# Moving batch 1's first projections ahead of the maxima, and the normalisations from ScalarE to GpSimd, in a decoder layer

## The chip, the core and the metric
The kernel runs on one NeuronCore of a Trainium2 chip. Its engines are TensorE (matmuls and transposes; PE in the profile, its weight loads PEld), VectorE (DVE), ScalarE (ACT), GpSimd (POOL) and SyncE (SP), which only issues copies here. Each runs its own list of instructions in order, and they meet at semaphores. "ACTq" and "SPq" are an engine's queue: what it issues or handles beside its arithmetic. The metric is the device time of one execution in microseconds; lower is better.

## What is computed
One decoder layer on x (4 batches, 256 rows, 256 channels) and a context of the same shape, all float32:

```
x = layernorm(x + attention(x))        # 32 heads of 8 channels, 8 key/value heads, biases
x = layernorm(x + wkv(w, u, k=x, v=ctx))
x = layernorm(x + ffn(x))              # ffn has a layernorm of its own, gamma and beta
attention: softmax(Q K^T / sqrt(8)) V, then Wo and bo
wkv:  a scan over the rows, per channel, with running maximum o:
      y = (exp(o-no) p + exp(u+k-no) v) / (exp(o-no) q + exp(u+k-no))
ffn:  layernorm(relu(x up_w)^2 down_w + (x expert_weight) * sum(top 2 of x gate_w)) * gamma + beta
```

## The kernel before
**Units.** The attention of a batch is cut into two groups of 128 query rows, so there are 8 groups, and a group into 16 units of two matmuls for maxima and one for exponentials. `maxima_unit` (L589) multiplies q by k for the query rows and VectorE takes the row maxima (L1180), negated. `exp_unit` (L605) multiplies k by q again, transposed, and ScalarE exponentiates into one of 8 `probs` buffers (L812). `pv_group` (L617) multiplies four of them by v. The exponential of a unit comes LAG = 15 units behind its maxima. While there are no exponentials yet, an idle matmul (L635) stands behind each maxima unit.

**Precision and rows.** q and k are split into three bfloat16 parts, and the six products that matter lie in rows 0 to 5 of every 8 partitions of `q_rows` and `k_rows` (BLOCKS, written by `q_row_copies` and `k_row_copies`, L486 and L492, as copies from `q_parts` and `k_parts`). Row 6 of `q_rows` takes the negated maxima of the group: VectorE's or GpSimd's `parts` (L1218, L1037) cut them in parts, TensorE transposes them (`m`, L692), VectorE or ScalarE takes them out (`mt`, L1228, L861), SyncE copies them into the row (`mc`, L550). There are two such parcels for each group. Every batch has its own `q_rows` and `k_rows`, set to zero and one by memsets, most of them on GpSimd. The row copies of a batch are issued by SyncE; for batch 0 some of them by ScalarE (L819, L824).

**Chunks.** Behind the attention each group of 128 rows is a chunk that goes through out projection, layernorm 0, the scan, layernorm 1, the feed-forward part and layernorms 2 and 3. WIDE is 6: chunks 0 to 5 are the early ones. For a layernorm k, VectorE takes statistics (`st`, L1145) and the variance (`var`, L1152, L1154), GpSimd raises it to the power -1/2 (`pow`, L1061); for an early chunk it also makes the negative mean (L1059) and the offset (L1066), and ScalarE normalises (`nor`, L794). The last two chunks are normalised by VectorE (L1160).

**Order.** All engines walk through the same ticks. The table `AT` gives each step of each batch, group or chunk a tick, and an engine's instructions are in the order of the ticks; units have theirs every R = 32 ticks from START = 1920, the exponentials 480 later. So the order of work on each engine, the SyncE queue with its loads (`load`) among it, is written out by hand or by a planner. `LOAD_AFTER` makes some loads wait for a count of maxima. The single PSUM bank `ps_a` is handed from use to use in the order of the ticks (A_BY). Before the first maxima unit TensorE waits for the parts and rows of batch 0 with 2, 12 and 2 idle matmuls between the waits.

Of the kernel before, what the change touches and what calls it, by code (L numbers as in the profile page):

```python
# [6 lines left out]
def decoder_layer(nc, x, x_cols, ctx_cols, w_qk, w_post, up_w, down_w, out):  # L7
    fp32, bf16 = mybir.dt.float32, mybir.dt.bfloat16
# [42 lines left out]
        "k": (1456, 2315, 2440, 3400),  # L51
        "kv": (-1, 2342, 2463, 3423),
        "k1": (1514, 2367, 2505, 3466),
        "kr": (1542, 2381, 2625, 3501),
        "vc": (1610, -1, -1, -1),
        "k2": (1580, 2527, 3002, 3551),
        "k3": (1661, 2784, 3522, 3773),
        "q0": (1503, 2379, 2792, 3624),
        "qs0": (-1, 2399, 2875, 3647),
        "qh0": (1561, 2540, 2904, 3685),  # L60
        "qr0": (1589, 2556, 3075, 3742),
        "qm0": (1618, 2603, 3177, 4479),
        "ql0": (1643, 2641, 3398, 4558),
        "q1": (1561, 2536, 2920, 3560),
        "qs1": (-1, 2559, 2975, 3583),
        "qh1": (1803, 2716, 3023, 4019),
        "qr1": (1831, 2748, 3052, 4075),
        "qm1": (1860, 2801, 3092, 4264),
        "ql1": (1885, 2922, 3110, 4538),
        "kc0": (1542, 2381, 3240, 4435),  # L70
        "kc1": (1634, 2637, 3618, 4606),
        "kc2": (1703, 2805, 3852, 4658),
        "qc00": (1644, 2556, 3102, 4698),
# [4 lines left out]
        "qc12": (1989, 3087, 3963, 4919),  # L78
        "load": (2110, 2145, 2179, 2324, 2683, 2857, 3075, 3295, 3839, 3867, 3910, 3941, 3993, 4675),
# [17 lines left out]
        "att": (3119, 3916, 4333, 4751, 5167, 5656, 6186, 6734),  # L97
        "att_e": (3135, 4030, 4319, 4735, 5182, 5662, 6175, 6760),
        "xbo": (2985, 3148, 3697, 4454, 5032, 5129, 5552, 6707),
# [1354 lines left out]
```

## Time and profile before

| what | value |
|---|---|
| median of 3 runs | 216.61 us (215.62 to 217.32) |
| the profiled execution | 216.79 us |
| its span, first to last instruction | 215.0 us |
| TensorE busy | 199.7 us (93%) |
| VectorE busy | 163.1 us (76%) |
| ScalarE busy | 150.9 us (70%) |
| GpSimd busy | 129.6 us (60%) |

Busy is time in which an instruction of the engine was running, by the profile; the ends of matmuls are modelled. The profiled execution is one run; what lies between its span and its time is start and end around the instructions.

### The profile page before, as it was taken

Reading aid. Unit: us, or ns where it says so; the run is one execution under the profiler, and the core shown is the slowest. Engines: PE = TensorE matmul, PEld = TensorE weight load, DVE = VectorE, ACT = ScalarE, POOL = GpSimd, SP = SyncE. Lnnn points to the kernel's source line nnn. Section 1 sums busy time; section 2 is a strip of 40 time slices with the busy share of each in tenths; the row PEclk is TensorE's granted clock in tenths of the full one; section 3 lists DMA queues with packets and bytes.
Section 4 is the critical chain, followed back from the end, with each engine's and each line's share of the span. In section 5 each row is a group of like instructions: output and inputs, shape, how many; then the busy total and the mean of one; then the engine's idle time right before and its main releaser. Section 6 shows DMA issues by size and latency. Waiting matters only on the chain.

```text
span 215.0 us, 4364 instructions
## 1 busy us (share of the span) xinstructions
PE 199.7 (93%) x1295; PEld 111.7 (52%) x1295; DVE 163.1 (76%) x392; ACT 150.9 (70%) x334; POOL 129.6 (60%) x256
## 2 busy tenths in 40 slices
PE   8889999979999899999999999999999998799970
PEld 3533543433433334575465445664655487698950
DVE  3469778778999899998979899976754837956274
ACT  2310477867899789989799879998967984763520
POOL 8995164753465724567476786867495493177622
PEclk9999999999999999999999999999999999999996
DMA  3145227943116602131000000010000000000001
GB/s 122 43 117 170 70 56 226 255 127 108 27 44 203 218 2 64 49 90 36 19 9 7 2 0 9 2 33 25 2 6 0 3 24 26 2 5 0 24 24 49
DMA packets 14759, 12.35 MB, mean 57 GB/s; under 512 B 3856, under 2 KB 12688, under 8 KB 14480
## 3 DMA queue, kind: packets, MB, share of 16 engines
q1 hardware_dynamic: 14064, 11.72, 19.0%
q10 hardware_dynamic: 672, 0.36, 0.6%
q8 instruction: 10, 0.16, 0.3%
q14 instruction: 13, 0.11, 0.2%
HBM read 6.57 MB, written 1.05 MB: 35 GB/s over the span
## 4 chain that ended last, share of the span: by engine, by line
PE 71%; DMA 8%; DVE 7%; ACT 6%; issue 5%; ACTq 1%; POOL 1%; POOLq 0%; DVEq 0%
PE ps_b L781 10%; PE ps_heads L629 10%; PE ps_exp L613 10%; PE ps_b L764 9%; DMA q_rows<-max_t 7%; PE ps_max L600 6%; PE ps_exp L635 4%; PE ps_exp L764 3%; PE ps_b L747 3%; PE ps_a L722 3%; PE ps_a L676 2%; ACT probs L812 2%; PE ps_a L665 2%; DVE maxima L1180 2%; PE ps_a L585 2%
## 5 line engine op out<-in xcount | busy, mean ns | idle before, releaser
L1180 DVE TENSOR_REDUCE maxima<-ps_max 128x2 f32<-128x512 f32 x128 | 85.0, 684 | 10.6 <-PE ps_max L600 9.7
L812 ACT ACTIVATE probs<-ps_exp 128x512 f32<-128x512 f32 x128 | 73.6, 599 | 14.6 <-PE ps_exp L613 14.1
L613 PE MATMUL ps_exp<-q_rows,k_rows 64*128 64x512 bf16 x128 | 46.2, 385 | 3.8 <-ACT probs L812 1.7
L600 PE MATMUL ps_max<-k_rows,q_rows 64*128 64x256 bf16 x256 | 47.4, 274 | 0.7 <-DMA q_rows<-q_parts 0.6
L613 PEld LDWEIGHTS ps_exp<-q_rows,k_rows 64*128 64x128 bf16 x128 | 11.4, 93 | 45.0 <-ACT probs L812 25.9
L629 PE MATMUL ps_heads<-probs,v_cols 128*32 128x512 f32 x256 | 33.9, 604 | 0.0
L781 PE MATMUL ps_b<-down_sb,inner_t 128*128 128x256 f32 x112 | 29.4, 388 | 0.7 <-ACT relu_t L943 0.7
L764 PE MATMUL ps_b<-x_t,up_sb 128*128 128x128 f32 x192 | 27.1, 285 | 1.1 <-DVE h L1367 1.1
L1061 POOL TENSOR_TENSOR rstd<-var_eps,minus_half 128x1 f32<-128x1 f32 x32 | 19.6, 611 | 11.7 <-DVE var_eps L1154 11.7
L764 PEld LDWEIGHTS ps_b<-x_t,up_sb 128*128 128x128 f32 x192 | 23.2, 191 | 6.0 <-issue 4.0
L781 PEld LDWEIGHTS ps_b<-down_sb,inner_t 128*128 128x128 f32 x112 | 19.4, 190 | 4.3 <-issue 1.5
L1145 DVE BATCH_NORM_STATS2 stats<-h 128x6 f32<-128x256 f32 x32 | 13.4, 422 | 8.1 <-POOL h L1129 7.7
L600 PEld LDWEIGHTS ps_max<-k_rows,q_rows 64*128 64x128 bf16 x256 | 14.6, 94 | 6.4 <-DVE maxima L1180 3.9
L1059 POOL TENSOR_SCALAR neg_mean<-mean_var 128x1 f32<-128x1 f32 x24 | 6.3, 262 | 17.9 <-DVE var_eps L1154 17.8
L1074 POOL TENSOR_TENSOR new_v<-wgt,ctx_t 128x256 f32<-128x256 f32 x14 | 10.4, 741 | 4.9 <-issue 3.9
L1037 POOL TENSOR_TENSOR maxima<-maxima 128x16 f32<-128x16 f32 x28 | 6.3, 225 | 9.6 <-DVE maxima L1180 8.4
L898 ACT ACTIVATE wgt<-delta,bonus_decay 128x128 f32<-128x128 f32 x32 | 10.9, 400 | 0.7 <-DVE delta L1276 0.5
L980 POOL MEMSET q_rows<- 128x4096 bf16 x3 | 10.5, 3511 | 0.0
L905 ACT ACTIVATE wgt<-wgt 128x512 f32<-128x512 f32 x16 | 10.2, 636 | 0.1
L1090 POOL TENSOR_TENSOR y_num<-wgt,num 128x256 f32<-128x256 f32 x8 | 5.6, 699 | 7.3 <-DVE num L1305 7.3
L949 ACT ACTIVATE inner_t<-relu_t 128x512 f32<-128x512 f32 x16 | 9.9, 627 | 0.1
L635 PE MATMUL ps_exp<-ident_bf 128*128 128x512 bf16 x31 | 9.5, 384 | 0.0
(129 smaller groups left out, 345.2 us busy)
## 6 DMA issues: line engine op xcount, KB each, us to landing
q_rows<-q_parts SPq DMA_DIRECT2D x46, 64.0 KB, 2.1
x_t<-in_x_cols SPq DMA_DIRECT2D x4, 256.0 KB, 3.3
x_in<-in_x SPq DMA_DIRECT2D x4, 256.0 KB, 4.5
ctx_t<-in_ctx_cols SPq DMA_DIRECT2D x4, 256.0 KB, 3.0
up_sb<-in_up_w SPq DMA_DIRECT2D x1, 1024.0 KB, 6.1
down_sb<-in_down_w SPq DMA_DIRECT2D x1, 1024.0 KB, 6.1
out_y<-y_out SPq DMA_DIRECT2D x8, 128.0 KB, 1.7
post_sb<-in_w_post SPq DMA_DIRECT2D x1, 906.0 KB, 5.5
```

The lines of the kernel that those rows point to most:

```text
L600: last = nc.tensor.matmul(ps_max[n % 2][:, r, :], q_rows[b][at:at + HALF, g, REP * jj + 2 * half + r, h * P:h * P + P], k_rows[b][at:at + ...
L613: nc.tensor.matmul(ps_exp[n % 2][:, :], k_rows[b][at:at + HALF, JH * g + jj, kt * P:kt * P + P], q_rows[b][at:at + HALF, g, REP * jj:REP * ...
L629: last = nc.tensor.matmul(ps_heads[s % 2][32 * j:32 * j + 32, :], flat(v_cols[b][:, :, :])[:, at:at + 32], probs[(4 * n + j) % 8][:, :], s ...
L635: nc.tensor.matmul(ps_exp[1][:, :], src[:, 0:P], src[:, 0:P].rearrange("p (a t) -> p a t", a=1) .broadcast_to([P, REP, P]), start=True, st ...
L764: last = nc.tensor.matmul(ffn_banks[k][:, v * n:v * n + n], up_sb[:, c, m * P:m * P + P], x2_t[:, c, columns_of(p)], start=(c == 0), stop= ...
L781: last = nc.tensor.matmul(down_part(p, i), inner_t[:, m, i * P:i * P + P], down_sb[:, m, :], start=(m == 0), stop=(m == NI - 1))
L812: nc.scalar.activation(probs[n % 8][:, :], ps_exp[n % 2][:, :], ACT.Exp, scale=SCALE).then_inc(s_exp, 1)
L898: last = nc.scalar.activation(wgt[:, 2 + i, c, cols], delta[:, c, cols], ACT.Relu, scale=sign, bias=bonus_decay[:, i, c:c + 1])
L980: gp.memset(q_rows[b][:], 0.0).then_inc(s_ones, 1)
L1061: gp.tensor_tensor(rstd[k][:, ti], var_eps[k][:, ti], minus_half[:, ti], ALU.pow).then_inc(s_rstd[k], 1)
L1145: own(nc.vector.bn_stats(stats[k][:, i, :], src[:, i, :]))
L1180: nc.vector.tensor_reduce(maxima[s % 2][:, g, j // JH, 0, at:at + 2], ps_max[n % 2][:, :, :], AX, ALU.max, negate=True).then_inc(s_max, 1)
```

## The change
- The k projection of batch 1 and its first q projection stand before the first maxima unit; x of batch 1 is loaded third, at once. Three idle matmuls each stand behind batch 1's k, batch 0's second q and batch 0's v; the 16 idle matmuls between the waits go.
- GpSimd normalises the six early chunks, four times each. VectorE no longer adds the epsilon for them, GpSimd does; negative mean and offset go.
- GpSimd issues the row copies of the second and third part of batch 0's k (three copies). ScalarE issues three q copies of set 0, SyncE the rest.
- There are three `q_rows` and `k_rows` instead of four. Batch 3 takes batch 0's place, after its exponentials, and a copy for each set clears row 6 first. `q_rows` 1 is cleared by VectorE.
- There are 12 `probs` buffers instead of 8.
- For group 0, GpSimd makes the parts of the maxima and ScalarE takes the transposed ones out (VectorE before); ScalarE takes out batch 0's v.
- All ticks are new. x of batch 1 leaves the list of loads; the steps named in the prediction are shown.

```diff
 AT
-        "k": (1456, 2315, 2440, 3400),
+        "k": (1474, 1618, 2440, 3304),
-        "kv": (-1, 2342, 2463, 3423),
+        "kv": (-1, 1678, 2463, 3327),
-        "k2": (1580, 2527, 3002, 3551),
+        "k2": (1588, 2286, 3037, 3707),
-        "q0": (1503, 2379, 2792, 3624),
+        "q0": (1520, 1820, 2792, 3624),
-        "qh0": (1561, 2540, 2904, 3685),
+        "qh0": (1605, 1913, 2872, 3687),
-        "qc01": (1771, 2697, 3344, 4508),
+        "qc01": (1698, 2314, 3617, 4825),
-        "qc02": (1737, 2830, 3655, 4911),
+        "qc02": (1762, 2779, 3568, 4878),
-        "qc10": (1831, 2869, 3550, 4417),
+        "qc10": (1989, 2849, 3684, 5037),
-        "qc11": (1931, 2937, 3184, 4896),
+        "qc11": (1894, 2680, 3312, 5017),
-        "load": (2110, 2145, 2179, 2324, 2683, 2857, 3075, 3295, 3839, 3867, 3910, 3941, 3993, 4675),
+        "load": (2165, 2199, 2234, 2617, 2917, 2945, 3124, 3380, 3584, 3652, 3839, 5410, 5430),
-        "vb": (1903, 2623, 2687, 4223),
+        "vb": (1795, 2687, 3007, 4095),
-        "mc0": (2311, 2785, 3329, 3804, 4393, 4880, 5290, 5906),
+        "mc0": (2287, 2797, 3297, 3824, 4367, 4810, 5374, 5850),
-        "mc1": (2534, 3055, 3532, 4102, 4591, 5104, 5640, 6183),
+        "mc1": (2534, 3050, 3553, 4079, 4640, 5120, 5671, 6080),
...
+    ROT = 3
+    NPROBS = 12
...
 SyncE
+            def rows_free(b):
+                sp.wait_ge(s_ones, ROT + (b >= 2))
+                if b == 1:
+                    sp.wait_ge(s_q1_zero, 1)
+                if b >= ROT:
+                    sp.wait_ge(s_exp, UNITS * TT * (b - ROT + 1))
...
+                                if b >= ROT and qp == 0:
+                                    sp.dma_start(row_block(q_rows[b % ROT][:, g], len(BLOCKS)),
+                                                 row_block(q_rows[1][:, g], len(BLOCKS) + 1)).then_inc(s_rows[b][g], 16)
...
 ScalarE
-                    if n >= 8:
-                        act.wait_ge(s_pv, (n - 8) // 4 + 1)
+                    if n >= NPROBS:
+                        act.wait_ge(s_pv, (n - NPROBS) // 4 + 1)
...
 GpSimd
+            for kp, done in ((1, s_k2), (2, s_k3)):
+                gp.wait_ge(done, 1)
+                k_row_copies(gp, 0, kp, s_krows_pool)
+            gp.memset(q_rows[2][:], 0.0).then_inc(s_ones, 1)
...
+            def normalise(k, p, src, dst, done):
+                gp.wait_ge(s_rstd[k], p + 1)
+                for i in CHUNKS[p][1]:
+                    last = gp.tensor_scalar(dst[:, i, :], src[:, i, :], mean_var[k][:, i, 0:1], rstd[k][:, i:i + 1],
+                                            ALU.subtract, ALU.mult)
+                last.then_inc(done, 1)
...
                             if p < WIDE:
-                                gp.tensor_scalar(neg_mean[k][:, ti], mean_var[k][:, ti, 0], -1.0, None,
-                                                 ALU.mult).then_inc(s_negmean[k], 1)
+                                gp.tensor_scalar(var_eps[k][:, ti], mean_var[k][:, ti, 1], EPS, None,
+                                                 ALU.add).then_inc(s_pool, 1)
+                                npool[0] += 1
+                                gp.wait_ge(s_pool, npool[0])
                             gp.tensor_tensor(rstd[k][:, ti], var_eps[k][:, ti], minus_half[:, ti],
                                              ALU.pow).then_inc(s_rstd[k], 1)
-                            if p < WIDE:
-                                gp.wait_ge(s_negmean[k], p + 1)
-                                gp.wait_ge(s_rstd[k], p + 1)
-                                gp.tensor_tensor(offset[k][:, ti], neg_mean[k][:, ti], rstd[k][:, ti],
-                                                 ALU.mult).then_inc(s_offset[k], 1)
...
 TensorE
-                    if n == 0:
-
-                        for done, value, n_idle in ((s_q2[0], 1, ROW_FILL), (s_q3[0], 1, 6 * ROW_FILL),
-                                                    (s_krows[0], 16 * len(BLOCKS), ROW_FILL)):
-                            pe.wait_ge(done, value)
-                            for k in range(n_idle):
-                                idle_matmul(ident_bf)
```

## Rows read from the trace of the kernel before

**Rows 1.** four stretches: busy us (count) by engine, granted TensorE clock, DMA share, GB/s
```profile
0.00:24.80 24.80, 22.36 (x94) 10.04 (x94) 15.25 (x29) 4.31 (x8) 18.93 (x30) 1.00 0.38 110
24.80:80.00 55.20, 51.28 (x374) 20.98 (x373) 47.46 (x92) 44.41 (x97) 28.61 (x64) 1.00 0.43 125
80.00:180.00 100.00, 99.10 (x668) 57.01 (x667) 80.21 (x208) 86.50 (x198) 66.83 (x133) 1.00 0.08 20
180.00:215.00 35.00, 26.90 (x166) 23.73 (x164) 20.17 (x65) 15.66 (x32) 15.23 (x29) 0.94 0.06 20
```

**Rows 2.** TensorE's waits, 24 to 80 us: in total, times, longest
```profile
PE ps_exp L613 <- ACT probs L812: 1.7, 7, 0.3
PE ps_exp L613 <- DMA q_rows<-max_t: 1.6, 2, 0.9
```

**Rows 3.** TensorE's waits, 80 to 215 us
```profile
PE ps_b L764 <- DVE h L1367: 1.1, 1, 1.1
PE ps_b L781 <- ACT relu_t L943: 0.7, 1, 0.7
```

**Rows 4.** timeline of the start: start us, us, engine, line, operation, count
```profile
9.12 3.63 PE L635 MATMUL ps_exp<-ident_bf 128*128 128x512 bf16 x16
...
13.29 0.38 PE L600 MATMUL ps_max<-k_rows,q_rows 64*128 64x256 bf16 x2 [0.55 <-DMA q_rows<-q_parts]
...
13.77 6.42 DVE L1180 TENSOR_REDUCE maxima<-ps_max 128x2 f32<-128x512 f32 x10
...
22.64 0.39 PE L600 MATMUL ps_max<-k_rows,q_rows 64*128 64x256 bf16 x2
...
23.29 0.39 PE L600 MATMUL ps_max<-k_rows,q_rows 64*128 64x256 bf16 x2
...
24.80 0.39 PE L600 MATMUL ps_max<-k_rows,q_rows 64*128 64x256 bf16 x2
```

**Rows 5.** timeline before the first unit, ScalarE and the queues
```profile
7.59 0.40 ACT L840 ACTIVATE k_parts<-kv_rest 64x256 bf16<-64x256 f32 x1
...
8.24 0.42 ACT L853 ACTIVATE q_parts<-q_rest 128x256 bf16<-128x256 f32 x1 [0.25 <-DVE q_rest L1194]
8.30 2.09 ACTq L495 DMA_DIRECT2D k_rows<-k_parts  x3
...
8.91 7.12 SPq L489 DMA_DIRECT2D q_rows<-q_parts  x10
...
10.49 1.22 ACTq L489 DMA_DIRECT2D q_rows<-q_parts  x2
11.75 0.47 ACT L849 ACTIVATE q_parts<-ps_heads,qk_sb 128x256 bf16<-128x256 f32 x1 [3.09 <-issue]
```

**Rows 6.** timeline of SyncE's queue, 15 to 26 us
```profile
17.88 0.43 SPq L518 DMA_DIRECT2D ctx_t<-in_ctx_cols  x1
21.41 0.54 SPq L550 DMA_DIRECT2D q_rows<-max_t  x1
```

**Rows 7.** the copies of line 550, issue to landing
```profile
DMA to landing us min/median/max: 1.8/1.9/3.8
```

**Rows 8.** groups of instructions: xcount, then busy us, mean ns, idle before
```profile
L794 ACT ACTIVATE x<-h,offset,rstd 128x256 f32<-128x256 f32 x12 | 7.2, 601 | 0.9 <-POOL offset L1066 0.7
...
L1059 POOL TENSOR_SCALAR neg_mean<-mean_var 128x1 f32<-128x1 f32 x24 | 6.3, 262 | 17.9 <-DVE var_eps L1154 17.8
...
L1066 POOL TENSOR_TENSOR offset<-neg_mean,rstd 128x1 f32<-128x1 f32 x24 | 4.6, 193 | 3.7 <-POOL rstd L1061 0.4
L1125 POOL TENSOR_TENSOR h<-h,post_sb 128x256 f32<-128x256 f32 x6 | 4.4, 730 | 2.1 <-ACT h L794 2.0
...
L1022 POOL CAST q_parts<-q_rest 128x256 bf16<-128x256 f32 x6 | 2.4, 394 | 0.1
```

**Rows 9.** chain that ended last, 24 to 80 us: start us, us, what
```profile
70.87 3.68 DMA q_rows<-max_t
```

**Rows 10.** GpSimd's waits, 24 to 200 us
```profile
POOL maxima L1037 <- DVE maxima L1180: 8.4, 7, 2.6
```

More of the change, by code:

```diff
@@ L263, in decoder_layer @@
         k_rest, v_t = [kv[0:KVD] for kv in kv_rest], [kv[KVD:2 * KVD] for kv in kv_rest]
-        q_rows = [sb(f"q_rows{b}", [P, NSET, HH, T], bf16) for b in range(B)]
-        k_rows = [sb(f"k_rows{b}", [P, NSET * JH, T], bf16) for b in range(B)]
+        q_rows = [sb(f"q_rows{i}", [P, NSET, HH, T], bf16) for i in range(ROT)]
+        k_rows = [sb(f"k_rows{i}", [P, NSET * JH, T], bf16) for i in range(ROT)]
         v_cols = [sb(f"v_cols{b}", [P, TT * NSET, GS * 32 + HS]) for b in range(B)]
@@ L275, in decoder_layer @@
         max_t = sb("max_t", [P, NSET, P], bf16)
-        probs = [sb(f"probs{i}", [P, REP * P]) for i in range(8)]
+        probs = [sb(f"probs{i}", [P, REP * P]) for i in range(NPROBS)]
         heads_t = [sb(f"heads_t{i}", [P, REP * P]) for i in range(2)]
@@ L310, in decoder_layer @@
         rstd = [sb(f"rstd{i}", [P, TT]) for i in range(4)]
-        neg_mean = [sb(f"neg_mean{i}", [P, TT]) for i in range(4)]
-        offset = [sb(f"offset{i}", [P, TT]) for i in range(4)]
         ps_max = [ps(f"ps_max{i}", [P, 2, T]) for i in range(2)]
@@ L357, in decoder_layer @@
         s_var = [sem(f"s_var{k}") for k in range(4)]
-        s_negmean = [sem(f"s_negmean{k}") for k in range(4)]
         s_rstd = [sem(f"s_rstd{k}") for k in range(4)]
-        s_offset = [sem(f"s_offset{k}") for k in range(4)]
         s_x1 = by_class("s_x1")
@@ L600, in maxima_unit @@
                     last = nc.tensor.matmul(ps_max[n % 2][:, r, :],
[L601 to L602 removed]
+                                            q_rows[b % ROT][at:at + HALF, g, REP * jj + 2 * half + r, h * P:h * P + P],
+                                            k_rows[b % ROT][at:at + HALF, JH * g + jj, :], start=True, stop=True)
                 last.then_inc(s_max_mm, 1)
@@ L667, in _ @@
                         last.then_inc(s_a, 1)
+                        if b == 1:
+                            for k in range(FILL):
+                                idle_matmul(ident_bf)
                     for g in range(NSET):
@@ L678, in _ @@
                             last.then_inc(s_q0 if b == 0 else s_a, 1)
+                            if b == 0 and g == 1:
+                                for k in range(FILL):
+                                    idle_matmul(ident_bf)
                     if AT["v"][b] == tick:
@@ L685, in _ @@
                         last.then_inc(s_a, 1)
+                        if b == 0:
+                            for k in range(FILL):
+                                idle_matmul(ident_bf)
                 for s in range(GROUPS):
@@ L837, in _ @@
                                              bias=bkv_sb[0:KVD, 0:1]).then_inc(s_k1, 1)
+                    if b == 0 and AT["vb"][0] == tick:
+                        act.wait_ge(s_const, 1)
+                        a_filled(act, ("v", 0))
+                        nc.scalar.activation(
+                            heads_of(v_cols[0])[:, :, :, 0:HD],
+                            ps_a[:, 0:TT * KVD].rearrange("p (x j d) -> p x j d", j=GS, d=HD), ACT.Copy).then_inc(s_a_read, 1)
                     if b == 0 and AT["k2"][0] == tick:
@@ L968, in _ @@
             gp.memset(k_rows[0][:], 1.0).then_inc(s_ones, 1)
-            for i in range(2):
-                gp.memset(maxima[i][:, :, :, PARTS:HD], 0.0).then_inc(s_zeros, 1)
             own(gp.memset(ident[:], 0.0))
@@ L975, in _ @@
             gp.tensor_copy(ident_bf[:], ident[:]).then_inc(s_ident, 1)
+            for i in range(2):
+                gp.memset(maxima[i][:, :, :, PARTS:HD], 0.0).then_inc(s_zeros, 1)
+            for b in range(1, ROT):
+                gp.memset(k_rows[b][:], 1.0).then_inc(s_ones, 1)
             own(gp.memset(v_cols[0][:], 0.0))
             gp.memset(heads_of(v_cols[0])[:, :, :, HD:HD + 1], 1.0).then_inc(s_const, 1)
+            gp.wait_ge(s_ones, 1)
+            for kp, done in ((1, s_k2), (2, s_k3)):
+                gp.wait_ge(done, 1)
+                k_row_copies(gp, 0, kp, s_krows_pool)
+            gp.memset(q_rows[2][:], 0.0).then_inc(s_ones, 1)
             for b in range(1, B):
-                gp.memset(k_rows[b][:], 1.0).then_inc(s_ones, 1)
-                gp.memset(q_rows[b][:], 0.0).then_inc(s_ones, 1)
                 own(gp.memset(v_cols[b][:], 0.0))
```

181 lines of the change are left out of this document (81 added, 100 removed), and 172 rows, old and new, of the table AT.

## The prediction

> **What bounds the kernel now.** I read the table of stretches first, then TensorE's waits, then the timeline of the first 25 us, and last the groups of instructions and the copies. The table [rows 1] shows TensorE busy 99.1 of the 100 us between 80 and 180, with VectorE at 80.2, ScalarE at 86.5 and GpSimd at 66.8: there the order and amount of TensorE's work is the time, and a faster ScalarE buys nothing by itself. The granted clock is 1.00 up to 180 (the 2.4 GHz level). Room is in three places. Before 24.8 TensorE is busy too, but partly with idle matmuls. From 24.8 to 80 it is idle 55.20 - 51.28 = 3.9 us. After 180 it is idle 8.1 us, nearly all in the last chunk's chain, whose code and order the change leaves as they are.
>
> Of the 3.9 us, TensorE's own waits name 1.7 us for ScalarE's exponentials and 1.6 us for the copy of the maxima into row 6 of `q_rows` [rows 2]; 0.6 us has small causes. Later only two waits stand out, 1.1 us for a VectorE sum and 0.7 us for ScalarE's ReLU [rows 3].
>
> **The first projections of batch 1.** Before, they stand among the first 15 maxima units. Two neighbouring units without a projection start 22.64 and 23.29, 0.65 apart; with one between them 23.29 and 24.80, 1.51 apart [rows 4]. One projection costs 0.86 us there, the two 1.7 us. The change puts k and q0 of batch 1 before the first unit, where TensorE now runs 16 idle matmuls for 3.63 us [rows 4] and then waits: the cover is long enough for both, with 9 idle matmuls left.
>
> **Does the first unit come earlier?** Now it starts at 13.29, 2.19 us after the last of five copies issued by ScalarE's queue: three k copies from 8.30, two q copies from 10.49, 0.61 each, so the last at 11.10 [rows 4, 5]. After, ScalarE issues three q copies alone, but k's second part is written before q's first (0.4 us more), which makes q's second part some 0.7 us later than the 8.24 of now [rows 5]. It ends at 8.24 + 0.7 + 0.42 = 9.36; a dispatch for batch 1 lies between, so the last of three issues starts at about 9.46 + 1.22 = 10.7, and the unit could start at 12.9. Set 0's copies are one half. The projection q0 of batch 1 must wait for ScalarE's new copy of v, behind those issues (until 11.3), 0.45 us, and takes 0.86 to 1.0: it ends at 12.7, just hidden. GpSimd now issues three k copies. No row shows one issued there; at ScalarE's 0.61 the third starts near 9.3, at double that near 10.5, and both land before 12.9: nothing.
>
> The other half is set 1, needed by the ninth unit. ScalarE starts its q at 11.75 now, and SyncE's ten q copies end at 8.91 + 7.12 = 16.03, so the last starts at 15.4 and is usable at 17.6, before the ninth unit at 13.29 + 8 x 0.643 = 18.4 [rows 4, 5]. After, q of set 1 stands behind the same three issues and the copy of v (11.75 again), but SyncE takes its second part first: q, rest and second part end at about 13.2, six issues of 0.61 start the last at 16.3, usable at 18.5. The ninth unit was due at 12.9 + 5.1 = 18.0. So the 0.4 us won at the first unit is lost at the ninth, which starts at 18.5, as now.
>
> **The first exponential.** From the ninth unit to it is 24.80 - 18.4 = 6.4 us now, and 4.7 without the two projections: 23.2. It also needs the first row copy of the maxima. Now that is issued at 21.41, the loads before it at 17.88 and earlier [rows 6]. After, SyncE meets three loads (x_in of batch 0, ctx of batch 0, x of batch 2) ahead of this copy, the first of which waits for the last q copy at 18.5. The row copy goes out near 21.0 behind 768 KB. A row copy lands in 1.8, 1.9 or 3.8 us (least, median, most) [rows 7]: 22.9 to 24.8. I take 23.6, between median and most: a gain of 24.8 - 23.6 = 1.2 us. Its ends are 1.65 (the copy is hidden) and 0 (it lands last at 24.8).
>
> **GpSimd normalises six chunks.** Four normalisations for each of six chunks, 24 activations in three groups of 12, 6 and 6 at 0.60 [rows 8], leave ScalarE: 14.3 us of its 150.9. The same operation on GpSimd has no row. Its nearest ones are the cast of one input, 0.39, and the sum of two, 0.73 [rows 8]; it has one tensor input and two scalars, so I take 0.47, the cast with the 0.07 by which a 128x1 TENSOR_SCALAR (0.262) stands over a 128x1 TENSOR_TENSOR (0.193) there. GpSimd gives up 24 products of 0.193 and exchanges one 0.262 for another: per normalisation +0.28 (bounds +0.20 and +0.54), together +6.7 us over some 190 us. It also drops three memsets at the start. It stays under TensorE's load [rows 1]. Per normalisation the path from variance to result loses a hop and 0.15 of VectorE's. All that is off TensorE's path in the 80 to 180 stretch: 0 there.
>
> **Twelve exp buffers, three places for rows, the new order.** With ScalarE shorter and exponentials allowed four more ahead of the products, some of the 1.7 us goes; with the weight loads moved against the row copies (the third chunk of the order puts `up_w` and x of batch 3 between two copies, `down_w` right behind one) some of the 1.6 us. The chain of waits has a row copy of 3.68 us at 70.87 that TensorE waits for [rows 9]. I take half of 3.3, 1.6 us; ends 0.5 and 2.6. After 80, 0.3 of the 0.7 for ReLU (0 and 0.7).
> Three places cost a new wait in SyncE: batch 3's rows wait for exponential 32 of 128. By the ticks it is due two units after that one, so what is queued behind it (the later row copies) is held for at most a unit: 0, and if it slips, up to 0.7 for TensorE. The copies that clear row 6 are two more on that queue, 0.6 each, hidden by slack of several units.
>
> **The sum.** 215.0 - 1.2 - 1.6 - 0.3 = 211.9 us of span. The profiled execution took 216.79 with a span of 215.0, so 1.79 lies around it: 213.7. The median of the three runs is 216.61, 0.18 below that execution: 213.5 us.
>
> **Rivals.** (A) All the room is taken: 1.65 + 3.9 + 0.7 = 6.25, so 210.4. For it: TensorE's other stretches show that it can run without gaps. Against: the waits of [rows 2] have several causes.
> (B) The moved work is given back to row copies: the first lands at 24.8 and the later ones stay as late; only 0.3 remains, 216.3. For it: SyncE has three loads in front of the first copy, and the longest landing is 3.8 [rows 7].
> (C) GpSimd's queue becomes the wait, the case on the other side. The parts of the maxima stand in it with the normalisations, and transpose, copy and exponentials hang on them. It is idle before these parts 7 times, 8.4 us [rows 10], for 14 parcels: seven come without a margin. If each of the seven stands behind one normalisation and its scalar step, 0.47 + 0.26 = 0.73, TensorE loses 5.1, against the 3.1 gained: 218.6. It decides once more than four of the seven are not covered. Against it: GpSimd waits 8.4 us in the others, and the parcels have slack of about four units.
> (D) The k copies issued by GpSimd land late. If an issue takes 1.8, three times ScalarE's, the third starts at 11.6, the first unit is at 13.8 and the ninth at 18.95: +0.45, so 214.0. The Trainium skill, SBUF — State Buffer, "SBUF: two separate sides", says of copies issued by GpSimd that their descriptors are made by that engine and are held up while VectorE runs in a two-port mode; no row of before has such a copy, so nothing here bears it out yet.
>
> **Chances.** The forecast 0.48, with its own range 211.8 (1.65 + 2.6 + 0.7) to 215.3 (0.8 + 0.5); A 0.09; B 0.20; C 0.15; D 0.08. For the range, from A's 210.4 to 217.5, part of the way to C, about 0.15 is left out. Faster by over 1% (which is about what a measurement can tell from no change) is under 214.4: most of the forecast (0.42), A and half of D: 0.55. Slower is over 218.8: the worse half of C and mishaps of B, 0.12. Within 1%: 0.33.
>
> **What would show it.** The first unit at about 12.9, the ninth at 18.5, the first exponential at 23.6 with a wait for the maxima's row copy ahead of it. TensorE's idle time from there to 80 near 2.3 us. ScalarE at about 137 us of busy time, GpSimd's normalisation at 0.47. TensorE's waits on the parts of the maxima (transposes, L692) would mean C; a first unit at 13.8 with the wait on the k rows, D. If the whole gain is there at 25 us and gone at 80, B. I am wrong altogether if TensorE's busy time in the later stretches grows by more small changes between its kinds of work, which no wait would show.

## The result and the profile after

The kernel after takes 222.11 us (221.18 to 222.24), the one before 216.29 in the same job: the ratio is 1.025 [1.019, 1.032], slower by 1.9 to 3.2%. Forecast were 213.5 us and a range of 210.4 to 217.5. The profiled execution took 221.18 us, with a span of 219.3 against 215.0. Times here are medians of undisturbed executions; one execution each of the kernel after, of e3 and of e14 was disturbed and is left out, and the profile of e3 is of that one.

The table below is read from the timelines, one profiled execution for each kernel: the start in us of the first, 65th, 97th, 113th and last of the 128 exponentials on ScalarE, and the span. The labelled kernels come in the next section.

| kernel | 1st | 65th | 97th | 113th | last | span |
|---|---|---|---|---|---|---|
| before | 25.3 | 84.8 | 124.6 | 147.5 | 170.1 | 215.0 |
| after | 22.8 | 80.5 | 120.7 | 148.3 | 171.2 | 219.3 |
| e9_copy_for_norm | 23.1 | 80.5 | 119.4 | 143.7 | 166.6 | 212.4 |
| e13_real_23 | 23.0 | 80.6 | 119.5 | 143.6 | 166.5 | 213.4 |
| e12_real_01 | 23.3 | 81.3 | 121.5 | 147.1 | 170.0 | 215.9 |
| e17_fill | 23.7 | 81.9 | 122.0 | 148.1 | 171.0 | 218.9 |
| e1_norm_on_act | 23.0 | 81.3 | 122.3 | 148.1 | 171.2 | 221.6 |

The kernel after is ahead by 2.5 us at the first exponential and by 4.3 at the 65th. It is behind by 0.8 at the 113th, and the tail from the last exponential to the end is 48.1 us instead of 44.9. One execution says little about tenths at the start. Ten kernels of the next section (all but e3, e7, e10 and e14) have the same start as the kernel after. In these eleven profiles the first unit lies between 12.2 and 13.3 us.

The start of the kernel after, timeline of TensorE, and SyncE's and GpSimd's copies (start us, us, engine, line, operation; answers to [rows 4] to [rows 6]):

```profile
10.68 0.82 PE L650 MATMUL ps_exp<-ident_bf 128*128 128x512 bf16 x3
11.33 1.03 PE L687 MATMUL ps_a<-x_t,qk_sb 128*128 128x256 f32 x4
12.34 0.38 PE L615 MATMUL ps_max<-k_rows,q_rows 64*128 64x256 bf16 x2
...
17.76 0.39 PE L615 MATMUL ps_max<-k_rows,q_rows 64*128 64x256 bf16 x2 [0.22 <-DMA q_rows<-q_parts]
...
22.40 0.39 PE L628 MATMUL ps_exp<-q_rows,k_rows 64*128 64x512 bf16 x1
...
20.15 0.54 SPq L565 DMA_DIRECT2D q_rows<-max_t  x1
...
7.69 1.80 POOL L496 DMA_DIRECT2D k_rows<-k_parts  x3 [2.13 <-ACT k_parts L848]
```

The first unit is at 12.34 (13.29 before), the ninth at 17.76, the first exponential unit at 22.40 (24.80 before). Three copies issued by GpSimd take 1.80 us, 0.60 each.

The stretches of the kernel after (columns as in [rows 1]):

```profile
24.80:80.00 55.20, 51.54 (x378) 20.96 (x377) 47.68 (x93) 43.40 (x96) 27.96 (x61) 1.00 0.44 124
...
80.00:180.00 100.00, 96.32 (x648) 56.83 (x647) 74.96 (x178) 77.20 (x177) 80.48 (x125) 0.98 0.07 18
180.00:219.00 39.00, 28.93 (x167) 25.13 (x166) 21.51 (x65) 13.18 (x28) 25.72 (x38) 0.92 0.06 21
```

Between 80 and 180 TensorE is busy 96.3 us instead of 99.1, GpSimd 80.5 instead of 66.8, and the granted clock is 0.98 instead of 1.00. What TensorE waits for in the kernel after, 24.8 to 80, 80 to 180 and 180 to 219 us (us in total, times, longest; answers to [rows 2, 3]):

```profile
PE ps_exp L628 <- ACT probs L819: 1.1, 5, 0.3
PE ps_a L600 <- POOL x L997: 1.1, 2, 0.6
PE ps_exp L628 <- DMA q_rows<-max_t: 0.9, 2, 0.5
...
PE ps_a L600 <- POOL x L997: 3.4, 5, 1.6
...
PE ps_a L600 <- DVE x L1185: 2.8, 2, 2.4
PE ps_b L781 <- DVE h L1377: 0.6, 1, 0.6
```

L600 are TensorE's transposes of a normalised x, L997 is GpSimd's normalisation, and L1185 VectorE's for the last two chunks. The waits for exponentials and row copies are 2.0 us instead of 3.3 (2.7 in e9_copy_for_norm and in e18), and a new wait for x stands beside them.

GpSimd's groups by form in the kernel after (columns as in [rows 8]):

```profile
L997 POOL TENSOR_SCALAR x<-h,mean_var,rstd 128x256 f32<-128x256 f32 x12 | 14.9, 1238 | 0.9 <-POOL rstd L1070 0.2
L997 POOL TENSOR_SCALAR y_out<-h,mean_var,rstd 128x256 f32<-128x256 f32 x6 | 7.7, 1279 | 0.9 <-POOL rstd L1070 0.7
L997 POOL TENSOR_SCALAR h<-h,mean_var,rstd 128x256 f32<-128x256 f32 x6 | 7.4, 1231 | 0.1
L1144 POOL TENSOR_TENSOR h<-h,post_sb 128x256 f32<-128x256 f32 x6 | 4.5, 743 | 0.5
```

One normalisation takes 1.23 to 1.28 us, 24 of them 30.0. The forecast took 0.47, and its upper bound, the sum of two tensors, was 0.73 (0.74 here).

How this reaches TensorE is seen best in the chain that ended last in the kernel after (start us, us, what), here the piece from 171 to 183 us:

```profile
172.10 0.57 POOL rstd L1070
...
172.87 1.25 POOL x L997
174.12 1.22 POOL h L997
...
175.42 0.73 POOL h L1144
...
176.23 0.73 POOL h L1148
176.96 0.69 POOL h L1060
177.64 0.69 POOL y_num L1112
178.33 1.21 POOL h L997
...
181.28 0.54 POOL rstd L1070
...
181.92 0.42 DVE x L1185
...
182.48 0.67 PE ps_a L600 x2
```

From 172.10 to 181.82 the chain is GpSimd's queue, with nearly no gap. The last chunk's rstd (181.28), which VectorE and then TensorE need, stands behind three normalisations of earlier chunks. Its step with the same work on VectorE takes 0.42 us. In the page's summary of the chain GpSimd has 23% of the span.

The granted clock (1.00 is the upper level, 0.50 the lower) falls to its lower level twice before the end, from 137.7 and from 182.0 us, 3.4 us each. In the kernel before it is at the upper level until 210.9. The mean granted clock of the kernel after is 0.977 to 0.979 in its three executions, of the kernel before 0.986 to 0.996. The stretches around both falls in the kernel after:

```profile
134.00:137.70 3.70, 2.03 (x18) 1.32 (x18) 2.69 (x4) 2.09 (x4) 3.51 (x7) 0.99 0.00 0
137.70:141.10 3.40, 3.38 (x16) 2.36 (x17) 2.07 (x6) 1.39 (x4) 3.05 (x7) 0.50 0.00 0
178.00:182.00 4.00, 2.03 (x17) 1.84 (x16) 2.48 (x7) 1.19 (x2) 3.84 (x6) 1.00 0.01 2
182.00:185.40 3.40, 2.92 (x9) 2.49 (x10) 2.25 (x7) 0.38 (x1) 1.90 (x3) 0.51 0.10 35
```

Ahead of each fall TensorE was busy about half of the time and GpSimd nearly all of it.

### The profile page after: what moved, and what is told of

Its sections match the earlier page's. It is cut to its first block, busy times and chain, and to the rows that moved or that the text cites. A ratio compares the mean times of both kernels' runs of the same rounds, so it can differ in the third digit from the quotient of the medians.

```text
span 219.3 us, 4290 instructions
## 1 busy us (share of the span) xinstructions
PE 199.5 (91%) x1288; PEld 113.2 (52%) x1288; DVE 162.1 (74%) x362; ACT 140.4 (64%) x313; POOL 150.2 (68%) x260
## 3 DMA queue, kind: packets, MB, share of 16 engines
q1 hardware_dynamic: 13984, 11.78, 18.5%
HBM read 6.57 MB, written 1.05 MB: 35 GB/s over the span
## 4 chain that ended last, share of the span: by engine, by line
PE 45%; POOL 23%; DVE 10%; issue 9%; ACT 5%; DMA 4%; SPq 2%; POOLq 1%; DVEq 0%; ACTq 0%
PE ps_b L798 7%; PE ps_heads L644 7%; PE ps_exp L628 7%; POOL x L997 5%; POOL rstd L1070 4%; PE ps_max L615 3%; DMA q_rows<-max_t 3%; PE ps_exp L650 3%; DVE maxima L1206 3%; PE ps_b L781 3%; PE ps_a L687 2%; ACT probs L819 2%; POOL h L997 2%; PE ps_a L600 2%; PE ps_b L764 2%
## 5 line engine op out<-in xcount | busy, mean ns | idle before, releaser
L1206 DVE TENSOR_REDUCE maxima<-ps_max 128x2 f32<-128x512 f32 x128 | 84.3, 682 | 13.5 <-PE ps_max L615 12.9
L819 ACT ACTIVATE probs<-ps_exp 128x512 f32<-128x512 f32 x128 | 73.3, 598 | 18.0 <-PE ps_exp L628 17.6
L798 PE MATMUL ps_b<-down_sb,inner_t 128*128 128x256 f32 x112 | 30.5, 399 | 0.0
L781 PEld LDWEIGHTS ps_b<-x_t,up_sb 128*128 128x128 f32 x192 | 24.1, 197 | 5.2 <-issue 2.5
L798 PEld LDWEIGHTS ps_b<-down_sb,inner_t 128*128 128x128 f32 x112 | 20.2, 198 | 3.9 <-issue 2.0
L1044 POOL TENSOR_TENSOR maxima<-maxima 128x16 f32<-128x16 f32 x32 | 7.1, 221 | 14.5 <-DVE maxima L1206 13.3
L997 POOL TENSOR_SCALAR x<-h,mean_var,rstd 128x256 f32<-128x256 f32 x12 | 14.9, 1238 | 0.9 <-POOL rstd L1070 0.2
L600 PE MATMUL ps_a<-ident,x 128*128 128x128 f32 x32 | 7.1, 306 | 7.3 <-POOL x L997 4.4
L807 ACT ACTIVATE x_t<-ps_a 128x256 f32<-128x256 f32 x16 | 6.1, 382 | 11.5 <-PE ps_a L600 11.3
L1066 POOL TENSOR_SCALAR var_eps<-mean_var 128x1 f32<-128x1 f32 x24 | 6.0, 252 | 8.6 <-DVE mean_var L1171 8.3
L870 ACT ACTIVATE max_t<-ps_a 128x128 bf16<-128x128 bf16 x16 | 4.4, 275 | 10.0 <-PE ps_a L709 9.9
```

Of the source, the lines that this page charges most:

```text
L600: last = nc.tensor.transpose(ps_a[:, c * n + k * P:c * n + k * P + P], src[:, i, c * P:c * P + P], ident[:, :])
L781: last = nc.tensor.matmul(ffn_banks[k][:, v * n:v * n + n], up_sb[:, c, m * P:m * P + P], x2_t[:, c, columns_of(p)], start=(c == 0), stop= ...
L798: last = nc.tensor.matmul(down_part(p, i), inner_t[:, m, i * P:i * P + P], down_sb[:, m, :], start=(m == 0), stop=(m == NI - 1))
L819: nc.scalar.activation(probs[n % NPROBS][:, :], ps_exp[n % 2][:, :], ACT.Exp, scale=SCALE).then_inc(s_exp, 1)
L997: last = gp.tensor_scalar(dst[:, i, :], src[:, i, :], mean_var[k][:, i, 0:1], rstd[k][:, i:i + 1], ALU.subtract, ALU.mult)
L1206: nc.vector.tensor_reduce(maxima[s % 2][:, g, j // JH, 0, at:at + 2], ps_max[n % 2][:, :, :], AX, ALU.max, negate=True).then_inc(s_max, 1)
```

## The experiments

Theory P: the price of a normalisation on GpSimd is the cause. Rivals: O, the new order or the ramp (the start, up to the first exponentials) is; K, the half clock is a large part of it. Ratios are against the kernel before in the same job. Differences of two kernels of different jobs are of their medians, and can be off by up to about 1 us: the kernel before took 216.1 to 217.2 in the five jobs.

**The normalisations on another engine.** e1_norm_on_act gives all 24 back to ScalarE in the kernel after:

```diff
 ScalarE
+            def normalise(k, p, src, dst, done):
+                act.wait_ge(s_offset[k], p + 1)
+                for i in CHUNKS[p][1]:
+                    last = affine(dst[:, i, :], src[:, i, :], k, i)
+                last.then_inc(done, 1)
...
 GpSimd
+                                    own(gp.tensor_scalar(neg_mean[k][:, ti], mean_var[k][:, ti, 0], -1.0, None,
+                                                         ALU.mult))
...
+                                gp.tensor_tensor(offset[k][:, ti], neg_mean[k][:, ti], rstd[k][:, ti],
+                                                 ALU.mult).then_inc(s_offset[k], 1)
...
-                        normalise(0, p, h1, x1[b % 2], s_x1[p >= WIDE])
```

> The changed kernel with the 24 early normalisations back on ScalarE; GpSimd adds epsilon, raises to the power and makes negative mean and offset; all ticks and all else as changed. Theory P (price: a normalisation on GpSimd takes 1.24 us in the changed trace, not 0.47, and GpSimd's queue became the wait): GpSimd's busy time falls from 150 to about 130 us, the lead of some 5 us that the changed kernel has at the maxima of unit 112 is kept to the end, 210 to 212 us. Rival O (the new order itself leaves gaps in the second half): the lead is lost all the same, 217 to 222. Rival S (it is ScalarE that needed the relief): above 216, with TensorE waiting for exponentials.

Measured: 223.02 us, ratio 1.028 [1.025, 1.030]. GpSimd's busy time is back at 129.8 us, ScalarE's at 151.1, and the time does not fall. It is above the ranges of both P and O. Rival S asked for waits on exponentials; they are 0.8 us from 24 to 80, less than the 1.7 of the kernel before. TensorE's waits from 80 us on in e1_norm_on_act:

```profile
PE ps_a L604 <- ACT x L815: 2.6, 4, 1.2
PE ps_b L785 <- DVE h L1398: 1.9, 1, 1.9
PE ps_heads L723 <- ACT heads_t L890: 1.1, 1, 1.1
PE ps_a L604 <- DVE x L1206: 0.9, 1, 0.9
```

The transposes now wait for ScalarE's x (a wait of 0.7 us for x_t and smaller ones are left out here). So the new order lets the normalisation on ScalarE be late too: it is no test of the price alone.

e2_norm01_on_act does so for layernorms 0 and 1 alone (`NOR_ACT = (0, 1)`), e4_norm_on_dve puts all four on VectorE (the branches for `nor0` to `nor3` lose `p >= WIDE` there and go from GpSimd), e15_split puts 0 and 1 on VectorE, 2 on ScalarE and leaves 3 on GpSimd.

> The changed kernel with layernorms 0 and 1 of the early chunks on ScalarE, 2 and 3 on GpSimd. TensorE's transposes wait for the results of 0 and 1 (4.4 us by name in the changed trace), not for 2 and 3. Theory P: most of the loss is in 0 and 1, so 213 to 218. Theory O: 217 to 221.

> The changed kernel with the early normalisations on VectorE, at 0.49 us each, at the same ticks. Theory P: GpSimd is freed of 30 us; VectorE gets 12 us, in a stretch where it is busy 75 to 90%: 211 to 216. Rival O: 219 or more. Against e1 it tells whether it matters which engine takes them, so long as it isn't GpSimd.

> A version for use: the changed kernel with layernorms 0 and 1 on VectorE (0.49 us each), 2 on ScalarE (0.60), 3 on GpSimd, where no engine waits for the result but the store. All of VectorE gave 218.2. Theory X: TensorE's waits for x are those of the VectorE version, the rest is lighter: 215.5 to 218. Below 215.5 it would beat both kernels.

Measured: e2 219.13 us, 1.011 [1.007, 1.016]; e4 218.21, 1.006 [1.003, 1.009]; e15 218.26, 1.008 [1.005, 1.011]. All three are 3 to 4 us better than the kernel after, and none reaches the kernel before. e2 is in the range of O and above that of P, e4 lies between the two, e15 is just above its range. No fall of the clock before the end shows in their profiled executions. In e4 the waits for x are shorter but not gone, and a wait for VectorE's h is longer:

```profile
PE ps_a L600 <- DVE x L1170: 2.9, 5, 1.0
PE ps_b L781 <- DVE h L1364: 1.8, 1, 1.8
```

**The normalisations alone in the kernel before.** e3_before_norm_on_pool moves the 24 to GpSimd there, with the code of the kernel after and one tick changed by two; VectorE still adds the epsilon.

> The kernel before with one part of the change alone: GpSimd normalises the six early chunks, at the ticks that ScalarE had (one tick moved from 4927 to 4929, behind its power). VectorE still adds epsilon. Theory P: 24 x (1.24 - 0.19) = 25 us more work for GpSimd in an order not made for it: clearly slower, 222 to 232. Rival O: within 2 us of before, since GpSimd is busy 60% there.

Measured: 222.61 us, 1.024 [1.020, 1.028]. The kernel before took 217.16 in that job, so this part alone costs 5.4 us without any other part of the change. The three executions behind this median have a mean granted clock of 0.994 to 0.996, as high as the kernel before: most of that loss needs no fall of the clock. The chief waits of TensorE from 80 us on in e3_before_norm_on_pool:

```profile
PE ps_a L585 <- POOL x L983: 2.0, 1, 2.0
PE ps_a L585 <- DVE x L1159: 1.4, 2, 1.0
```

**The price by form.** e5_forms leaves out a part of the arithmetic of the normalisation in the kernel after, or puts constants in its place, to see the price of each form:

```diff
-                    last = gp.tensor_scalar(dst[:, i, :], src[:, i, :], mean_var[k][:, i, 0:1], rstd[k][:, i:i + 1],
-                                            ALU.subtract, ALU.mult)
+                    if k % 2:
+                        last = gp.tensor_scalar(dst[:, i, :], src[:, i, :], 0.5, 1.25, ALU.subtract, ALU.mult)
+                    else:
+                        last = gp.tensor_scalar(dst[:, i, :], src[:, i, :], mean_var[k][:, i, 0:1], None, ALU.subtract)
```

> What a normalisation on GpSimd costs by its form. The changed kernel, but layernorms 0 and 2 of the early chunks only subtract the mean (one scalar read from memory) and leave the factor out; 1 and 3 subtract and multiply with two constants in the instruction. If each operation costs, 0.7 to 0.9 for the one and 1.24 for the other; if it is reading scalars, 0.8 and 0.4; if it is VectorE in the way, both still near 1.2. The time lies between the changed kernel's and e1's.

GpSimd's groups in e5_forms:

```profile
L998 POOL TENSOR_SCALAR x<-h 128x256 f32<-128x256 f32 x6 | 6.5, 1089 | 0.6 <-POOL rstd L1072 0.2
...
L1000 POOL TENSOR_SCALAR x<-h,mean_var 128x256 f32<-128x256 f32 x6 | 5.6, 938 | 0.4
```

Two operations with constants take 1.09 us, one with a scalar from memory 0.94, two with scalars from memory 1.24. So the second operation and the scalars each have a part, but one operation alone is already above the sum of two tensors. The time is 218.61, ratio 1.0075 [1.004, 1.011].

This run also gives a price of the clock. Of its eight executions three had a mean granted clock of 0.983 to 0.985 and took 219.66 to 219.84 us; five had 0.991 to 0.995 and took 218.03 in the mean (217.12 to 218.79). The difference, 1.7 us, is half of one stretch of 3.4 us. Other kernels give less for the same step of the mean clock: 0.9 us in e9 (one execution at 0.984), 0.8 in e18 (one at 0.985) and 0.1 in e1 (two at 0.981 and 0.983 against two at 0.995). So the price of a fall is not one number; these cases give nothing to 1.7 us.

**The price taken away.** e9_copy_for_norm leaves the arithmetic out and puts a copy in the place of each normalisation, on GpSimd at the same place in its list:

```diff
-                    last = gp.tensor_scalar(dst[:, i, :], src[:, i, :], mean_var[k][:, i, 0:1], rstd[k][:, i:i + 1],
-                                            ALU.subtract, ALU.mult)
+                    if src is dst:
+                        last = gp.tensor_copy(dst[:, i, 0:128], src[:, i, 128:256])
+                    else:
+                        last = gp.tensor_copy(dst[:, i, :], src[:, i, :])
```

> The changed kernel with the 24 normalisations on GpSimd replaced by plain copies of the same tile (the arithmetic of these normalisations is left out; layernorm 2's copies half a tile). Same engine, same place, same waits; a copy should take 0.4 us, about what the prediction gave a normalisation. So it shows what the changed kernel would be if its price had been as predicted. Theory P (the price alone explains it): 211 to 213. Theory O (the new order leaves gaps for TensorE, whichever engine normalises, as e1 and e4 hint, both no faster than before): 215 to 218. In both GpSimd's busy time is near 130.

Measured: 214.36 us, 0.990 [0.987, 0.993], 7.8 below the kernel after. That lies between the ranges, 1.4 above P's and 0.6 below O's. GpSimd's groups, TensorE's waits from 80 us on and the stretch from 80 to 180 in e9_copy_for_norm:

```profile
L1000 POOL COPY x<-h 128x256 f32<-128x256 f32 x12 | 4.8, 398 | 0.5 <-POOL rstd L1072 0.2
...
PE ps_b L781 <- DVE h L1379: 1.8, 1, 1.8
PE ps_a L600 <- DVE x L1187: 0.9, 1, 0.9
...
80.00:180.00 100.00, 98.85 (x668) 59.20 (x667) 78.52 (x188) 78.72 (x182) 69.13 (x130) 1.00 0.07 20
```

At about the price that the forecast assumed (0.40 for 0.47), the waits for GpSimd's x are gone, the clock holds, and the time is 0.9 us above the forecast. VectorE's busy time is 161.6 us here and 162.1 in the kernel after, so the loss is not a slower VectorE. P is shown for the 7.8 us; what is left for O is the 1.7 us that e9 loses behind its 65th exponential by the table.

**Which normalisations.** e12_real_01 and e13_real_23 are e9 with the real operation for layernorms 0 and 1 (`if k in (0, 1)`), or for 2 and 3. Theory X: the waits for the results of 0 and 1 are nearly all of it. Theory Q: any such work in GpSimd's queue costs the same.

> Which of the normalisations cost the time. The changed kernel with those of layernorms 0 and 1 as they are (1.24 us on GpSimd) and those of 2 and 3 replaced by copies (their arithmetic left out). With all four replaced it took 214.4, with none 222.2. Theory X (TensorE's transposes wait for the results of 0 and 1 themselves): nearly all of the 7.8 us is back, 220 to 222. Theory Q (any 10 us of work more in GpSimd's queue delays all that stands in it): half of it, 217 to 219.

> The other half: 0 and 1 replaced by copies, 2 and 3 real. Theory X: 214.5 to 215.5, nothing waits long for layernorms 2 and 3. Theory Q: 217 to 219, the same as its counterpart.

Measured: e12 217.53, 1.006 [1.004, 1.008]; e13 215.23, 0.996 [0.992, 1.000]. e12 is where Q put it and e13 where X put it, so neither theory fits both. Layernorms 0 and 1, whose results TensorE transposes, cost 3.2 us, and 2 and 3 cost 0.9. Together they cost 7.8, so 3.7 us is not the sum of the parts (3.4, 1.3 and 3.0 by the ratios). TensorE's waits from 80 us on in e12_real_01:

```profile
PE ps_a L600 <- POOL x L998: 2.8, 5, 1.0
PE ps_b L781 <- DVE h L1382: 1.8, 1, 1.8
```

**Is the rest the clock?** e17_fill and e18_fill_last keep TensorE busy in the two waits ahead of the falls (e18 has `{7: 10}` alone):

```diff
                         open_a(("x1", p))
+                        for k in range({5: 7, 7: 10}.get(p, 0)):
+                            nc.tensor.matmul(ps_a[:, :], ident_bf[:, 0:P], ident_bf[:, 0:P].rearrange("p (a t) -> p a t", a=1)
+                                             .broadcast_to([P, REP, P]), start=True, stop=True)
                         chunk_done(pe, s_x1, p)
```

> The kernel after with idle matmuls (128x512 bf16, into the bank that the transposes overwrite) ahead of TensorE's wait for x in the transposes L600 of chunks 5 (seven) and 7 (ten). There TensorE waited 1.55 and 2.44 us, and the granted clock fell to half for 3.4 us just behind. Ten of the earlier idle matmuls took about 2.2 us, so they lie inside the wait. Theory K (of the 7.8 us that the price of the normalisation costs, 3.2 + 0.9 are waits and pace, and the rest is the two stretches at half clock, which come because TensorE stands idle): no stretch at half level before the end, time 222.2 - 3.4 = 218.8 us, ratio to before about 1.01. Rival W (the 3.7 us is from the two layernorm pairs delaying each other on GpSimd, and the clock has no part): the clock may or may not fall, time 222 us. Rival X (the idle matmuls delay the transposes): above 222.2.

> The same with idle matmuls at chunk 7 alone (ten). Theory K: the stretch at half clock near 137.7 us stays, the one near 182 us goes; 222.2 - 1.7 = 220.5 us. Rival W: 222 us. If the stretch at 182 us only moves to a later place, K is right on the mechanism but the time stays at 222.

Measured in one job with the kernel before: e17 220.63, 1.020 [1.016, 1.023]; e18 220.15, 1.017 [1.013, 1.021]. They are 1.5 and 2.0 us below the kernel after, where K expected 3.4 and 1.7. By the ratios it is 1.2 and 1.8, and the intervals overlap with that of the kernel after, so the gain is likely and not settled. The profile of e17 shows no fall before the end, and the mean clock of all its executions is 0.989 to 0.992. The profile of e18 shows none near 138, although the same wait of 1.55 us stands there, but one from 188.5; the mean clock of its other three executions is 0.991 to 0.996. The wait in e18_fill_last, then the waits of TensorE after 80 us in e17_fill:

```profile
138.03 0.41 PE L600 MATMUL ps_a<-ident,x 128*128 128x128 f32 x2 [1.55 <-POOL x L1000]
...
PE ps_b L784 <- DVE h L1380: 1.8, 1, 1.8
PE ps_a L600 <- POOL x L1000: 1.8, 4, 0.7
```

Without the fall at 182 the wait for VectorE's h is 1.8 us, in the kernel after it was 0.6: 1.2 us of what the second fall took from TensorE seems to have lain inside a wait that is there anyway. So some 1.2 to 2.0 us of the 3.0 to 3.7 go with the falls. The rest, 1.0 to 2.5, stays in e17 with the clock up. The table of milestones puts about 1.0 of it in the tail: from the last exponential to the end it is 47.9 us in e17, 45.9 in e12, 46.9 in e13 and 45.8 in e9, and of e17's 2.1 over e9 the layernorms 2 and 3 by themselves are 1.1 (e13). Another 0.6 lies before the 113th exponential, which comes 124.4 us behind the first in e17 and 123.8 in e12. In the tail earlier chunks' normalisations stand on GpSimd ahead of the last chunk's rstd, as in the chain above.

**The ramp and the order.** e14_copy_no_ramp is e9 with all of batch 1's projections, their splitting into parts and their row copies at the ticks of before, and 11 more idle matmuls behind batch 0's v. Of the ticks two are shown:

```diff
-        "k": (1474, 1618, 2440, 3304),
+        "k": (1474, 2315, 2440, 3304),
-        "q0": (1520, 1820, 2792, 3624),
+        "q0": (1520, 2379, 2792, 3624),
...
-                            for k in range(FILL):
+                            for k in range(FILL + 11):
```

> What the moved projections are worth where nothing takes it back. The changed kernel with all four normalisations replaced by copies (214.4 us), and the whole projection column of batch 1 at the ticks of before; the idle matmuls behind its k are left out, 11 more stand behind batch 0's v. The prediction's step: two projections of 0.86 us back among the first units, 1.2 to 1.7 us: 215.6 to 216.4. Rival: the first exponential is later but TensorE, full behind it, makes up for it elsewhere: 214.2 to 215.

Measured: 217.68, 1.006 [1.004, 1.008], 3.3 us above e9 and above the range. The early column of batch 1 as a whole is worth more than the two projections of 0.86 that it takes out from among the units. In e14 the first exponential is at 24.1 (23.1 in e9), but the 33rd at 55.1 (52.1), with a wait of 1.1 us for q's row copies that e9 does not show. TensorE's wait in e14_copy_no_ramp:

```profile
PE ps_max L615 <- DMA q_rows<-q_parts: 1.1, 1, 1.1
```

From the first exponential to the 65th e14 takes 59.8 us, e9 57.4 and the kernel before 59.5.

e7_before_ramp does the ramp alone in the kernel before: x of batch 1 at once, its k and q0 ahead of the first unit (the ticks above, in the other direction).

> The kernel before with the first part of the change alone: x of batch 1 is loaded third, k and q0 of batch 1 are projected before the first maxima unit; rows, normalisations and every other tick as before. Theory: the first exponential starts 1.2 to 2.4 us earlier than 24.8, and since the old order keeps TensorE full from 80 to 180, most of it is kept: 214 to 215.5. Rival: the gain is given back before 80 us, at the copies of the maxima: 216 to 217.5.

Measured: 225.21, 1.039 [1.033, 1.046], above both ranges. TensorE in e7_before_ramp, timeline and a stretch:

```profile
13.06 2.08 PE L677 MATMUL ps_a<-x_t,qk_sb 128*128 128x256 f32 x4 [3.24 <-DVE v_cols L1210]
14.92 4.91 PE L636 MATMUL ps_exp<-ident_bf 128*128 128x512 bf16 x16
19.76 0.39 PE L601 MATMUL ps_max<-k_rows,q_rows 64*128 64x256 bf16 x2
...
10.70:17.50 6.80, 4.44 (x11) 2.25 (x12) 1.11 (x3) 1.37 (x3) 6.74 (x5) 0.50 0.36 92
```

The q projection waits 3.24 us for VectorE to take v out of `ps_a`, and TensorE runs at the lower level from 10.7 to 17.5. The 16 idle matmuls of before, which the change takes out, still stand behind it and take 4.91 us, and the first unit slips to 19.76. From the first unit to the end the kernel takes 202.3 us, before it took 201.7. So the early projections did not pay without the small parts of the change (v on ScalarE, no idle matmuls between the waits, the other copies); which of them is needed was not separated.

e10_new_front_old_chunks takes e1 and gives the chunks the ticks of the kernel before.

> As e1 (changed kernel, normalisations on ScalarE), but the ticks of everything behind the rows (parts of the maxima, products, chunks) are those of before; the projections, row copies, loads, three places and 12 buffers are the new ones. Against e1 (223.0) it differs in the order of the second part alone. Theory O (new order of parts and chunks costs): 211 to 215, all of the lead kept, no fall of TensorE's clock before the last 10 us. Theory P or a cost of three places: 220 or more.

Measured: 221.66, 1.023 [1.020, 1.026], against 223.02 for e1. Its 65th exponential is at 85.9, 4.6 us later than in e1, and its last at 172.9, 1.7 later. The old order of the chunks loses in the middle and wins at the end: its tail is 46.9 us and e1's 50.4. The time is in the range of "P or three places", but no normalisation is on GpSimd here, and e9 has three places too and is fast. So e10 leaves open what costs it 5 us; that the new order as such is the loss it does not show. The twelve buffers and the three places were not run by themselves.

## Why the prediction was wrong

**What bounds the kernel: right, with one gap.** TensorE in the middle, the ramp and the tail are where time moved. But the tail was taken as left alone by the change, and it grew from 44.9 to 48.1 us (45.8 in e9), because work of earlier chunks stands ahead of the last chunk's steps.

**The projections: right, too low.** Two times 0.86 was the size of the instructions. e14 measures 3.3 for the move together with the splitting and the row copies that hang on it.

**The first and the ninth unit: right within the spread.** 12.34 for 12.9 and 17.76 for 18.5; the eleven profiles with this start have 12.2 to 13.3 and 17.6 to 18.8. GpSimd's three issues took 0.60 each, so D was not there. What the Trainium skill, SBUF — State Buffer, "SBUF: two separate sides", says of copies issued by GpSimd is neither borne out nor contradicted; no stretch here shows such a copy held up.

**The first exponential: right in kind, above the bound.** The gain is 2.4 us, the forecast was 1.2 with bounds 0 and 1.65. From the ninth unit it took 4.6 us, as forecast (4.7); the rest is the ninth unit, 0.7 earlier. The row copy was issued at 20.15, not near 21.0, and TensorE's weight load waited 0.30 us for it. The eleven profiles have the first exponential unit at 22.2 to 23.6, where 23.6 was forecast.

**GpSimd normalises six chunks: this step failed.** The term "I take 0.47" measured 1.24, above the bound of 0.73. Both bounds were rows of other operations: the cast reads one tensor and the sum two, but neither is a TENSOR_SCALAR. The only row of that kind was the 128x1 one, 0.262 against 0.193 of a TENSOR_TENSOR, and its extra 0.07 was carried over as a constant, while at 256 columns the extra over the cast is 0.84. Per normalisation the net is not +0.28 but about 1.24 - 0.19 = +1.05; 24 of them make +25 us. GpSimd's busy time rose from 129.6 to 150.2, with three memsets less at the start. ScalarE's fell to 140.4, not to about 137: it takes over three copies, and its neighbouring instructions overlap, so that the 14.3 us were not all its own. "Off TensorE's path: 0 there" failed with it, as e9 shows: at 0.40 it is 0 there, at 1.24 TensorE is busy 2.5 us less between 80 and 180.

**Twelve buffers and the new order: right in size, not shown in cause.** From the first to the 65th exponential it takes 59.5 us before, 57.7 after and 57.4 in e9: 1.8 to 2.1 gained, forecast 1.6. But e14 has the buffers and the order of the chunks too, without the early column of batch 1, and takes 59.8: the gain hangs on that column, and was not theirs alone. "Idle time near 2.3 from 24.8 to 80" failed: 3.7, of which 1.1 is the wait for x.

**The sum.** e9's span is 212.4 for the forecast 211.9. By the table: 2.2 to the first exponential and 2.1 to the 65th are gained, then 0.5 to the 113th, 0.3 to the last and 0.9 in the tail are lost. That e9 comes so near is partly luck: its gains are 1.2 above the forecast 3.1, and its 1.7 of losses were taken as nothing. In the kernel after the last three are 5.1, 0.3 and 3.2: 215.0 - 2.5 - 1.8 + 5.1 + 0.3 + 3.2 = 219.3. Two slips of the sum itself change nothing here: the lower end of the forecast's own range is 211.7, not 211.8, since the 0.18 was left out, and the 0.8 in its upper end has no row and does not fit the bound of 0 given for the ramp.

**Rival C: the right mechanism at the wrong place.** GpSimd's queue became the wait. But it was looked for at the parts of the maxima, whose slack had a row [rows 10]; for these GpSimd still waits 8.1 us, 7 times, and no wait of TensorE from 24 us on names them. The path that had no slack was pow, normalise, transpose (L600), on which the moved work itself lies, and in the tail the last chunk's pow behind it. C's time, 218.6, was worked out with 0.73 for a step, and the range to 217.5 left that time out.

**The clock: no step of the forecast had it.** A wait of TensorE can cost more than its own length when the clock falls behind it, here up to 1.7 us for a fall (e5) and nothing in e1. Of the 7.8 us that the price costs, 4.1 to 4.7 are the two pairs by themselves, 1.2 to 2.0 go with the falls, and 1.0 to 2.5 come of both pairs together. That last part is read from the milestones and the chain; no run isolates it. Open too is why the new order with ScalarE normalising (e1) takes 223 us: its waits from 80 us on name ScalarE's x, heads and x_t for 4.4 us. Its profile shows one fall of 3.4 us from 189.4, but that is not the reason, since its executions with a mean clock of 0.995 take 223.0 too.

## What to carry to other kernels

Price a moved operation by a row of the same operation at the same size; if there is none, a row of another operation is no bound, and the first experiment is one instruction of it. When work moves into a queue, look first at the path that the moved work itself lies on and at what stands behind it in that queue near the end, and only then at the neighbours whose slack the profile happens to show. A cheap stand-in at the same place in the list (here a copy) separates the price of an operation from the order around it, which moving it to a third engine did not. It shows a cause and gives no usable kernel: of the versions that compute the layer fully, none beat the kernel before, and e4 with 218.21 came nearest.

## What the runs showed of the hardware

GpSimd's operations on 128x256 float32: copy 0.40 us, sum of two tensors 0.74, one operation with a scalar from memory 0.94, two with constants 1.09, two with scalars from memory 1.24. ScalarE's activation with both scalars took 0.60 [rows 8], and VectorE's normalisation 0.41 to 0.56 (groups of the kernels before and after and of e4). The Trainium skill, GPSIMD Engine Reference, "4.1 Engine selection", says that two-input elementwise work is about twice as slow as on VectorE and that one-input work runs at roughly line rate. For two inputs this case is near it: the product for y_num took 0.73 us on GpSimd and 0.43 on VectorE in the kernel before. For one input it differs: the TENSOR_SCALAR takes two to three times VectorE's time and is dearer than the sum of two; the measurement decides.

Two falls of the granted clock to the lower level, 3.4 us each, came near the end of waits of TensorE of 1.55 and 2.44 us in the kernel after. In e18 the same wait of 1.55 us brought none, and the wait of 1.8 us for VectorE's h was followed by a fall in e18 and by none in e17. So the wait alone does not tell whether a fall comes.
